# Preln transformer block pair, first attention: a lead of five turns, DVE-turned maxima, tile-wise norm scaling

## What is computed

```python
q = (x @ Wq.T).reshape(b, t, 8, 64)
kv_latent = x @ Wkv_down.T                       # 64 wide
k = (kv_latent @ Wk_up.T).reshape(b, t, 8, 64)
v = (kv_latent @ Wv_up.T).reshape(b, t, 8, 64)
scores = einsum('bqhd,bkhd->bhqk', q, k) * 64 ** -0.5
out = einsum('bhqk,bkhd->bqhd', softmax(scores), v)
x = x0 + out.reshape(b, t, 512) @ Wo.T           # x above is layernorm(x0)
```

## Time and profile before

| What | Before |
|---|---|
| Median of 3 runs (lowest, highest) | 2362.17 us (2358.39, 2366.94) |
| The profiled execution: its time | 2364.05 us |
| The profiled execution: its span | 2362.0 us |
| Mean granted TensorE clock (share of full speed) | 0.992 |
| PE (TensorE) busy | 2304.0 us (98%) |
| DVE (VectorE) busy | 1381.4 us (58%) |
| ACT (ScalarE) busy | 1469.0 us (62%) |
| POOL (GpSimd) busy | 1041.4 us (44%) |

### The profile page before, as it was taken

One profiled execution on the slowest core, in us unless ns is written; L12 is line 12 of the kernel. 1 busy time (PEld: TensorE's weight loads), 2 busy tenths in 40 slices (PEclk: granted clock), 3 DMA queues, 4 the chain that ended last, 5 costly groups with the idle time before them and its releaser, 6 DMA issues.

```text
span 2362.0 us, 39370 instructions
## 1 busy us (share of the span) xinstructions
PE 2304.0 (98%) x14921; PEld 1418.0 (60%) x14921; DVE 1381.4 (58%) x2122; ACT 1469.0 (62%) x2049; POOL 1041.4 (44%) x674
## 2 busy tenths in 40 slices
PE   7999999999998999999999999999999999999999
PEld 5445555555545888888888886444344444443688
DVE  5666665666653134222222324889889989899364
ACT  5777777777764344444444443678678778778643
POOL 1776776776775355645645745130000000000354
PEclk9999999999999999999999999999999999999999
DMA  2213213212204456555555556342333333332232
GB/s 62 68 48 99 82 55 100 82 55 90 82 21 139 143 177 195 181 170 196 196 171 190 183 172 185 103 110 75 86 75 68 96 71 70 94 83 48 77 109 80
DMA packets 156840, 259.06 MB, mean 110 GB/s; under 512 B 37004, under 2 KB 97292, under 8 KB 156300
## 3 DMA queue, kind: packets, MB, share of 16 engines
q1 hardware_dynamic: 156652, 256.53, 36.4%
HBM read 206.52 MB, written 60.68 MB: 113 GB/s over the span
## 4 chain that ended last, share of the span: by engine, by line
PE 62%; ACT 2%; DVE 1%; DMA 1%; issue 1%; SPq 1%; POOL 0%; POOLq 0%; DVEq 0%
PE m_R L130 46%; PE m_O L130 11%; PE m_X L130 4%; ACT m_P L1796 1%; DMA m_K<-bounce_k 1%; DVE m_mraw L1948 1%; PE m_X L227 1%; SPq L1654 0%; ACT m_OS L1803 0%; PE m_X L2162 0%; DVE m_ln_x L206 0%; PE m_R L227 0%; DMA inverses<-m_rinv 0%; SPq L1681 0%; DVE m_ln_stat L184 0%
## 5 line engine op out<-in xcount | busy, mean ns | idle before, releaser
L1948 DVE TENSOR_REDUCE m_mraw<-m_R 128x2 f32<-128x1024 f32 x512 | 622.8, 1221 | 72.0 <-PE m_R L130 60.8
L1796 ACT ACTIVATE m_P<-m_R 128x1024 f32<-128x1024 f32 x512 | 523.9, 1025 | 153.0 <-PE m_R L130 152.8
L130 PE MATMUL m_O<-m_P,m_V 128*17 128x256 f32 x4096 | 331.1, 395 | 4.5 <-ACT m_P L1796 2.5
L777 DVE CUSTOM_DVE_ANT_0 a_excess<-a_X,a_excess 128x512 f32<-128x512 f32 x256 | 166.5, 688 | 207.0 <-PE a_X L130 204.8
L943 POOL TENSOR_TENSOR a_accp<-a_accp,a_P 128x1024 f32<-128x1024 f32 x96 | 261.1, 2720 | 14.6 <-ACT a_P L628 5.4
L2053 POOL TENSOR_TENSOR m_act0l<-m_xf,m_act0h 128x512 fp32r<-128x512 f32 x128 | 164.9, 1291 | 209.4 <-ACT m_xf L1858 111.3
L628 ACT ACTIVATE a_P<-a_S 128x1024 f32<-128x1024 f32 x256 | 249.4, 1037 | 8.5 <-PE a_S L130 8.5
L130 PE MATMUL m_R<-m_act0h,wt 128*128 128x512 f32 x640 | 251.3, 393 | 0.0
L130 PE MATMUL a_O<-a_P,a_V 128*64 128x512 f32 x1024 | 251.0, 612 | 0.0
L130 PE MATMUL m_R<-m_act0l,wt 128*128 128x512 f32 x640 | 250.4, 391 | 0.0
L130 PE MATMUL m_R<-m_Q,m_K 64*128 64x512 f32 x800 | 201.3, 499 | 2.3 <-DVE m_mraw L1948 2.0
(11 more groups left out here) (271 smaller groups left out, 4172.6 us busy)
## 6 DMA issues: line engine op xcount, KB each, us to landing
wt<-wcopy SPq DMA_DIRECT2D x176, 512.0 KB, 3.4
m_K<-bounce_k SPq DMA_DIRECT2D x96, 128.0 KB, 5.5
m_ln_x<-x SPq DMA_DIRECT2D x23, 512.0 KB, 4.0
a_tile<-in_L_ffn_tiles SPq DMA_DIRECT2D x22, 512.0 KB, 3.6
wcopy<-in_L_ffn_tiles SPq DMA_DIRECT2D x22, 512.0 KB, 5.0
x<-xres SPq DMA_DIRECT2D x78, 128.0 KB, 2.6
m_Q<-bounce_q SPq DMA_DIRECT2D x150, 64.0 KB, 2.2
xres<-x SPq DMA_DIRECT2D x64, 128.0 KB, 2.7
```

The costliest lines, as they stand in the source:

```text
L130: return pe.eng.matmul(out, lhsT, rhs, start=start, stop=stop, skip_group_check=True)
L777: dve.eng.tensor_tensor_reduce(excess[:, h, :], bank(key), excess[:, h, :], 1.0, LOWEST, ALU.add, ALU.max, mraw[u % 2][:, q, h:h + 1]).the ...
L1796: act.eng.activation(P[h % 4][:, :, :], pair(key)[:, :, :], ACT.Exp, scale=SCALE).then_inc(R.free(key))
L1948: dve.eng.tensor_reduce(mraw[u % 2][:, at, :], pair(key)[:, :, :], AX.X, ALU.max).then_inc(R.free(key))
```

## The change

AHEAD becomes 5. The maxima are no longer turned by TensorE: VectorE negates them by a reduction over an axis of length 1 into a 128 x 32 tile and transposes that in 32 x 32 blocks. Rows of one head then lie in four blocks, and `move_rows` issues 8 DMAs (2 heads by 4 blocks; each 4 partitions by 32 elements) where it issued 2. `max_rows`, `keep_rows` and their place in the ring go. `move_rows` for unit u+1 is now at j = 3, and in SP's loop it stands behind `move_inverse`. The norm's steps spread over turns 8 to 21, with one tile scaled by ScalarE in each of turns 14 to 21. An output tile is prepared at j = 3 and projected in the next turn, j = 0, where the query is. Ahead of the loop the second query and the values move in between the maxima, the key differences behind them. `low_all` and `low_top` become columns of `lows`.

```diff
-    NH, NG, NP, AHEAD = 2, 4, 6, 6
+    NH, NG, NP, AHEAD = 2, 4, 6, 5
...
-        at = (13, 14, 17, 18, 19, 20, 21)
-        return (b + 1, at.index(n)) if n in at and (b + 1 < B or at.index(n) in (0, 1, 4, 5)) else None
+        at = (8, 9, 10, 11, 12, 14, 15, 16, 17, 18, 19, 20, 21)
+        return (b + 1, at.index(n)) if n in at and (b + 1 < B or at.index(n) in (0, 1, 4, 5, 6, 7, 8)) else None
...
     def rows_at(u, j):
-        return u + 1 if j == 2 and u + 1 < NU else None
+        return u + 1 if j == 3 and u + 1 < NU else None
...
-        return divmod(u - 6, NT) if j == 1 and u >= 6 else None
+        return divmod(u - 5, NT) if j == 3 and 5 <= u < NU - 3 else None
...
-        out += [("q", 0), ("halves", 0), ("q", 1), ("values", 0)]
-        for n in range(2 * AHEAD):
-            out += [("max", n, h) for h in range(NH)] if n % 2 else []
-            out += [("differ", 0, 1), ("differ", 0, 0), ("rows", 0)] if n == NT - 1 else []
+        out += [("q", 0), ("halves", 0)]
+        for n in range(1, 2 * AHEAD, 2):
+            out += [("max", n, h) for h in range(NH)]
+            out += [("q", 1)] if n == 1 else [("values", 0)] if n == 3 else []
+        out += [("differ", 0, 1), ("differ", 0, 0)]
...
             def move_rows(u):
-                sp.wait_ge(*X.emptied(("rows", u)))
+                sp.wait_ge(s_turned, u + 1)
                 sp.wait_ge(s_scores, NT * (u - 2))
...
                 for h in range(NH):
-                    sp.eng.dma_start(f32(M[u % 3][64 * h:64 * h + 1, :]), f32(mrow[u % 2][4 * h:4 * h + 4, :])).then_inc(s_rows[u % 3], 16)
+                    to = M[u % 3][64 * h:64 * h + 1, :].rearrange("o (q i r) -> o i q r", q=4, i=4)
+                    for i in range(4):
+                        part = slice(32 * i + 4 * h, 32 * i + 4 * h + 4)
+                        sp.eng.dma_start(f32(to[:, i, :, :]), f32(mrow[u % 2][part, :])).then_inc(s_rows[u % 3], 16)
...
-                if rows_at(u, j):
-                    move_rows(rows_at(u, j))
                 if sums_at(u, j) is not None:
                     move_sums(sums_at(u, j))
                 if j == 2 and u:
                     move_inverse(u - 1)
+                if rows_at(u, j):
+                    move_rows(rows_at(u, j))
...
-                    half = norm_at(u, j)[1] - 5
-                    norm.scale_act(act, norm_at(u, j)[0], 4 * half, 4 * half + 4)
+                    tile_of_norm = norm_at(u, j)[1] - 5
+                    norm.scale_act(act, norm_at(u, j)[0], tile_of_norm, tile_of_norm + 1)
...
-                    if u:
-                        dve.wait_ge(*X.filled(("rows", u - 1)))
-                    dve.eng.tensor_scalar(mneg[:, :, :], mraw[u % 2][:, :, :].rearrange("p q h -> p h q"), -1.0, None, ALU.mult).then_inc(s_max)
+                    dve.wait_ge(s_fill, 6)
+                    dve.wait_ge(s_turned, u)
+                    halved = mraw[u % 2][:, :, :].rearrange("p q (h k) -> p h q k", k=1)
+                    dve.eng.tensor_reduce(mneg[:, 0:NH * 4].rearrange("p (h q) -> p h q", h=NH), halved, AX.X, ALU.max, negate=True).then_inc(s_max)
+                    if u >= 2:
+                        dve.wait_ge(s_rows[(u - 2) % 3], 128 * ((u - 2) // 3 + 1))
+                    dve.wait_ge(s_max, u + 1)
+                    dve.eng.transpose(f32(mrow[u % 2][:, :]), f32(mneg[:, :])).then_inc(s_turned)
...
             def scores(n):
...
-                pe.wait_ge(s_rows[u % 3], 32 * (u // 3 + 1))
+                pe.wait_ge(s_rows[u % 3], 128 * (u // 3 + 1))
```

More of the change, by code:

```diff
@@ L349, in x_order @@
             out += [("values", values_at(u, j))] if values_at(u, j) else []
-            out += [("rows", rows_at(u, j))] if rows_at(u, j) else []
             out += [("differ", *differ_at(u, j))] if differ_at(u, j) else []
@@ L382, in attention_a @@
         accd, accp = [p.sb(f"accd{i}", [128, NH, 512]) for i in range(2)], p.sb("accp", [128, NH, 512])
-        mrow = [p.sb(f"mrow{i}", [NH * 4, 128], F32R) for i in range(2)]
+        mrow = [p.sb(f"mrow{i}", [128, 32], F32R) for i in range(2)]
         total = p.sb("total", [128, 256])
@@ L393, in attention_a @@
         mraw = [p.sb(f"mraw{i}", [128, NT // 2, NH]) for i in range(2)]
-        mneg = p.sb("mneg", [128, NH, 4], F32R)
+        mneg = p.sb("mneg", [128, 32], F32R)
         norm.small_tiles(p)
-        lows, low_all, low_top = p.sb("lows", [128, LOWS]), p.sb("low_all", [128, 1]), p.sb("low_top", [1, 1])
+        lows = p.sb("lows", [128, LOWS + 2])
+        low_all, low_top = lows[:, LOWS:LOWS + 1], lows[0:1, LOWS + 1:LOWS + 2]
         s_copy, s_tile, s_tile_hi, s_low = p.sem("copy"), p.sem("tile"), p.sem("tile_hi"), p.sem("low")
@@ L405, in attention_a @@
         s_lathi, s_qhi, s_max = p.sem("lathi"), p.sem("qhi"), p.sem("max")
-        s_rows = [p.sem(f"rows{i}") for i in range(3)]
+        s_rows, s_turned = [p.sem(f"rows{i}") for i in range(3)], p.sem("turned")
         s_scores, s_exp, s_pv, s_os = p.sem("scores"), p.sem("exp"), p.sem("pv"), p.sem("os")
@@ L487, in move_rows @@
             def move_rows(u):
-                sp.wait_ge(*X.emptied(("rows", u)))
+                sp.wait_ge(s_turned, u + 1)
                 sp.wait_ge(s_scores, NT * (u - 2))
                 if u < 3:
-                    sp.wait_ge(s_fill, 7)
+                    sp.wait_ge(s_fill, 8)
                 for h in range(NH):
-                    sp.eng.dma_start(f32(M[u % 3][64 * h:64 * h + 1, :]), f32(mrow[u % 2][4 * h:4 * h + 4, :])).then_inc(s_rows[u % 3], 16)
+                    to = M[u % 3][64 * h:64 * h + 1, :].rearrange("o (q i r) -> o i q r", q=4, i=4)
+                    for i in range(4):
+                        part = slice(32 * i + 4 * h, 32 * i + 4 * h + 4)
+                        sp.eng.dma_start(f32(to[:, i, :, :]), f32(mrow[u % 2][part, :])).then_inc(s_rows[u % 3], 16)
             def move_sums(u):
@@ L611, in keep_values @@
                 act.eng.activation(V[b % 2][:, :, :], bank(key).rearrange("p (t n) -> p t n", t=NT), ACT.Copy).then_inc(X.free(key))
[L613 to L618, removed]
             def exponent(n):
@@ L656, in scalar @@
             norm.scale_act(act, 0, 0, NT // 2)
+            for i in range(4):
+                norm.turn_act(act, 0, i % 2, i // 2)
             act.wait_ge(s_prod, 1)
@@ L661, in scalar @@
                     act.eng.activation(to, psS[i][:, k, 0:256].rearrange("p (g n) -> p g n", g=NG), ACT.Copy).then_inc(s_whi)
-            for i in range(4):
-                norm.turn_act(act, 0, i % 2, i // 2)
             for half in range(2):
                 latent_high(0, half)
-            for u in range(2):
-                query_high(u)
-            keep_values(0)
+            query_high(0)
             def way_high(i):
@@ L686, in scalar @@
                     surplus(n, h)
[L687 to L690, removed]
+                if n == 0:
+                    query_high(1)
+                if n == 2:
+                    keep_values(0)
+            for half in (1, 0):
+                differ_high(0, half)
             for m, (u, j) in enumerate(turns()):
@@ L705, in scalar @@
                     keep_values(values_at(u, j))
-                if rows_at(u, j):
-                    keep_rows(rows_at(u, j))
                 if differ_at(u, j):
@@ L736, in vector @@
                 dve.eng.memset(f32(M[i][:, :]), 0.0).then_inc(s_fill)
+            dve.eng.memset(f32(mneg[:, :]), 0.0).then_inc(s_fill)
             dve.wait_ge(s_fill, 2)
@@ L828, in judge @@
                     dve.wait_ge(s_low, LOWS)
-                    dve.eng.tensor_reduce(low_all[:, :], lows[:, :], AX.X, ALU.max).then_inc(s_low)
+                    dve.eng.tensor_reduce(low_all[:, :], lows[:, 0:LOWS], AX.X, ALU.max).then_inc(s_low)
                 else:
@@ L846, in vector @@
             norm.scale(dve, 0, NT // 2, NT)
+            for i in range(4):
+                norm.turn_dve(dve, 0, i % 2, i // 2)
             for i in range(2):
@@ L851, in vector @@
                     dve.eng.tensor_tensor(to, psS[i][:, k, 0:256].rearrange("p (g n) -> p g n", g=NG), hi, ALU.subtract).then_inc(s_wlo)
-            for i in range(4):
-                norm.turn_dve(dve, 0, i % 2, i // 2)
             for half in range(2):
                 latent_low(0, half)
+            keep_halves(0)
             query_low(0)
-            keep_halves(0)
-            query_low(1)
             def way_low(i):
@@ L867, in vector @@
                 reduce(n)
-                if n == NT - 1:
-                    for half in (1, 0):
-                        differ_low(0, half)
+                if n == 1:
+                    query_low(1)
+            for half in (1, 0):
+                differ_low(0, half)
             pending = None
@@ L1039, in maxima @@
                     ins.then_inc(s_early)
[L1041 to L1045, removed]
             def scores(n):
@@ L1127, in tensor @@
             key_halves(0)
-            query(1)
-            pe.wait_ge(s_identr, 1)
```

(10 more changed lines are left out.)

## The result

| | Before | After |
|---|---|---|
| Median | 2362.0 us (4 runs, 2358.39 to 2366.94) | 2564.75 us (4 runs, 2560.66 to 2567.65) |
| Ratio, 95% interval | | 1.085 (1.083 to 1.087) |
| Span of the profiled execution | 2362.0 us | 2563.2 us |
| Mean granted TensorE clock | 0.992 | 0.956 |

The change makes the kernel 8.5% slower, 203 us. 2591 us were forecast, with a range of 2500 to 2680 us.

What follows compares the result with a forecast made beforehand. TensorE's path was taken to bound the kernel: 2364.05 + 191 (waits for rows) + 60 (clock) - 5 (turning) - 17 (scaling) = 2593 us, or 2591 us against the median; range 2500 to 2680 us.

Steps and rivals of the forecast that it cites:

- The mechanism and its place: First attention: TensorE waits 5 to 8 us per unit before its first scores, for rows issued behind SP's inverse.
- The size of the wait: Before a unit's scores: 6.3 us for units 1 to 30, 2.4 us for unit 0's rows, together +191 us.
- T+15.1: T is the start of TensorE's turn j = 2; rows were wanted at T+8.2 and forecast to land at T+14.5.
- The clock: TensorE's matmuls slow down around each wait: 2.0 us lost, 30 times, +60 us; bounds 0 and 2.5 us each.
- Scaling tile by tile: Norm on ScalarE: one tile per turn leaves nothing of TensorE's waits for surplus, -17 us; at worst none gained.
- Outputs beside queries: Output projection moved to j = 0: same matmuls, no cost of its own; shortens turn j = 2 by 1.5 us.
- The turning: Maxima turned on VectorE: max_rows leaves TensorE, 0.16 us 31 times, -5 us in the loop; ahead of it about 0.
- The Trainium skill's rule on the ports: VectorE's negation: 0.19 us as a reduction; were the rule wrong, 0.9 us more per unit, 27 us in all.
- Cheap issues: Rival, SP's queue: eight smaller pieces issue faster, at 0.2 us a wait of 3.1 us per unit, about 2463 us; 6%.
- The inverse not in front: Rival, SP's queue: SP passes the inverse before VectorE's turning, 2.4 us paid per unit, about 2434 us; 4%.
- the rows in time: Rival, SP's queue at j = 3: the last DMA lands by T+8.2, no stall, only gains stay, 2340 us; 5%.
- Worse: Rival: strided pieces at 0.89 us and the negation as slow as before, 8.9 us per unit, 2682 us or more; 5%.

Runs made afterwards that it cites:

- a_lead6: The changed kernel with AHEAD = 6 again and nothing else: 2565.10 us, 1.084 of the kernel before.
- a_front: The changed kernel with move_rows at j = 2 ahead of move_sums and move_inverse, eight DMAs kept: 2396.79 us, 1.014 of the kernel before.
- a_four: The changed kernel with the same data moved into M by four DMAs per unit instead of eight: 2448.01 us, 1.037 of the kernel before.
- a_four_front: The changed kernel with four DMAs per unit and move_rows at j = 2 ahead of move_sums and move_inverse: 2332.53 us, 0.987 of the kernel before.
- a_two: The changed kernel with two of the eight DMAs into M per unit, the other six left out: 2406.81 us, 1.018 of the kernel before.
- b_norm: The kernel before with the norm's part alone (earlier statistics, one tile scaled per turn in turns 14 to 21): 2344.99 us, 0.992 of the kernel before.
- b_out: The kernel before with the outputs' part alone (prepared at j = 3, projected at j = 0): 2361.95 us, 0.998 of the kernel before.
- a_out_back: The changed kernel with the outputs' part taken back (prepared at j = 1, projected at j = 2): 2531.89 us, 1.071 of the kernel before.
- a_scalar: The changed kernel with four DMAs, move_rows ahead of the inverse, and the negation by tensor_scalar again: 2359.78 us, 0.999 of the kernel before.

## Why the prediction was right, point by point

**The mechanism and its place: right.** One wait of TensorE per unit, ahead of the unit's first scores, ended by the DMA into `M`, with SP's eight issues directly behind L518. `a_lead6`, `a_front`, `a_four` and `a_four_front` show it from four sides: an earlier turning changes nothing, another order takes away 130.4 of 166.9 us of waits, half the issues 86.5 us, and both together all.

**The size of the wait: a term too large.** 191 us were forecast, 164.1 us were measured in the loop. For units whose turns j = 2 and j = 3 are plain, 7.85 us together, 6.3 us was rather low: eleven of them lie between 5.3 and 7.9 us, 6.7 in the mean. The mis-sized step is "so it is 3.91 us long like j = 3, and so is the next one", taken for all units. In 19 others the two turns hold side work (transposes, key differences, values) and last 8.0 to 11.0 us; the rows are wanted later, and the wait is 3.8 to 5.6 us. The last one is the wait ahead of unit 1, with no inverse in front: 1.7 us for 2.4.

In the plain units the way of the sums was longer than forecast: in the mean the sums are read back 2.5 us after their write (forecast 2.1), the first row is issued 2.1 us after that (1.6), and the scores start 6.2 us later (6.3), at T+15.1 (14.5). The write varies with what SP issued ahead of it. With the 512 KB weight copy (L532) at j = 2, some 2.5 us ahead, it took 2.55 us to land in the mean of 22 units (1.4 to 4.0), and 1.4 us in each of the 9 units without. The waits of plain units are 7.2 us in the mean with the copy and 5.5 us without. In `a_four_front`, where the rows go in between, the same 22 writes took 1.5 us in the mean. No run leaves the copy out, so its part isn't taken apart.

**The clock: right.** Up to the next stage TensorE is busy for 756.6 us, and for 689.8 us in `a_four_front`, the version without waits, with the same matmuls; the mean granted clock there is 0.89 and 0.99. The slower matmuls cost 66.8 us by this, 2.1 us per wait. By subtraction it is 61.8 us, 1.9 us per wait: the change starts the next stage 228.7 us later (950.7 for 722.0), and 166.9 us of this are waits for `M`. 2.0 us each and 60 us in all were forecast. The subtraction gives 1.2 us per wait in `a_four` (2.7 us each) and 0.7 in `a_two` (1.8 us each): a shorter wait costs less clock too.

**Scaling tile by tile: right**, 17 us forecast, 17.0 shown alone by `b_norm`. **Outputs beside queries: right** as to their own cost (`b_out`) and as to the 1.5 us by which they shorten turn j = 2 (`a_out_back`).

**The turning: right in the loop, missed ahead of it.** `a_four_front` has its next stage 9.4 us before that of `b_norm`. 4.3 us of this arise ahead of the loop, which was put at nothing: turn 1 begins there at 40.39 us, against 44.66 in `b_norm`. (In the change it begins at 44.65: a wait of 2.79 us for `M` and slow matmuls take the gain.) The other 5.1 us arise in the loop, where 5 us were forecast for `max_rows`; no run takes `max_rows` apart from the rest of the change. The transposition takes 0.21 us, and the negation 0.16 us.

**The sum.** Forecast were 191 + 60 - 5 - 17 = 229 us. Measured at the start of the next stage are 166.9 + 61.8 - 9.4 - 17.0 = 202.3 us. Most of the difference is the wait.

**The Trainium skill's rule on the ports** ("SBUF — State Buffer", "Who interferes with whom"), that a `tensor_scalar` can contend with GpSimd and a `tensor_reduce` doesn't: the traces agree in both halves. As a `tensor_reduce` the negation takes 160 to 165 ns in all 32 places of `a_four_front`, beside whatever GpSimd does; as a `tensor_scalar`, in `a_scalar`, it takes 0.17 to 2.16 us in the same place, and the long ones end with a GpSimd operation. Its worth was mistaken: I priced it as 0.9 us more on the way of the rows, and in `a_scalar` the largest part was a wait of ScalarE for the norm.

**The rivals.** Cheap issues: no, 573 ns at the median for 512 bytes. The Trainium skill gives some 50 ns for the sequencer's part on GpSimd's issuing path ("DMA: Bandwidth & Descriptors", "Anatomy of one DMA — SWDGE (gpsimd) path"). By this row that isn't what a DMA holds SP's queue for. The inverse not in front, and the rows in time: these are what `a_front` and `a_four_front` had to be written for. Worse: no, the issues weren't dearer than forecast, and the negation was fast.

## What to carry to other kernels

A queue executes in order, and a step that waits for a round trip (here: write, wait until it has landed, read back) delays everything behind it by the whole trip. Before moving a small urgent transfer, write out the queue's timeline from its release to its deadline, with every issue at its own duration and with what newly comes in between, not only with what leaves. Count DMAs, not bytes, when they are small: merging eight into four halved their time on the queue.

## What the runs showed of the hardware that I had not expected

- A DMA over eight partitions that fills two rows (`a_four`) holds SP's queue for 0.52 us, one over four partitions that fills one row for 0.57 us.
- A 128 x 8 negation whose own work is 0.17 us took up to 2.16 us as `tensor_scalar`, the long ones until just after a GpSimd `tensor_tensor` had ended, and never over 0.17 us as `tensor_reduce`. This one difference moved the kernel by 27 us.
- The small write of the sums to DRAM landed after 1.4 us, and after 2.55 us in the mean where a 512 KB copy had been issued some 2.5 us ahead of it.
- In the change's 30 waits of 3.8 to 7.9 us the granted clock fell to 0.50 between 1.9 and 5.1 us after TensorE had stopped, three times only after it had started again, and stayed there for 2.9 to 6.2 us of its work. So a wait of 5.2 us in the mean was paid once as idle time and again with some 2 us in slow matmuls.
